# Output projection in three products of split operands, narrower heads of V, shared buffers and three moved steps in a transformer layer

## The reference

```python
q = x @ wq + x @ Aq @ Bq * 4; k = x @ wk; v = x @ wv + x @ Av @ Bv * 4   # 16 heads of 16
q, k = apply_rope(q), apply_rope(k)
attn = softmax(where(causal, -1e9, q @ k.T / 4))
x = layernorm(x + (attn @ v) @ wo)
h = gelu(butterfly(x @ W_exp + b_exp, up_weights) + up_bias)             # 1024 wide
x = layernorm(x + butterfly(h, down_weights) @ W_con + b_con + down_bias)
```

## Time and profile before

| what | value |
|---|---|
| median of 3 runs | 1165.44 us (1160.27 to 1165.82) |
| the profiled execution | 1159.63 us |
| its span | 1157.8 us |
| mean granted TensorE clock | 0.962 of full speed |
| PE, DVE, ACT, POOL busy | 1060.2, 875.7, 722.2, 570.2 us |
| 16 DMA engines | 147 GB/s on average |

### The profile page before, as it was taken

How to read it: one execution, slowest core, us unless ns; L and a number is a source line. 1 busy time by engine, 2 the same in 40 slices (tenths; PEclk the granted TensorE clock), 3 DMA queues, 4 the chain that set the end, 5 groups by cost and what they waited for, 6 DMA issues and landing times.

```text
span 1157.8 us, 28819 instructions
## 1 busy us (share of the span) xinstructions
PE 1060.2 (92%) x8974; PEld 787.9 (68%) x8974; DVE 875.7 (76%) x1950; ACT 722.2 (62%) x1113; POOL 570.2 (49%) x567
## 2 busy tenths in 40 slices
PE   5687879999999999999999999999999999999877
PEld 4464556767677776768677776768677776767566
DVE  6679977787777878787777778787777778776445
ACT  2186649475775758575775758575775758474613
POOL 2443526456382736456382836456382736443311
PEclk8788889999999999999999999999999999998989
DMA  7765553746465573646465573656465573651211
GB/s 275 158 207 117 163 131 93 197 122 193 98 211 129 160 185 117 192 118 201 91 210 129 154 192 113 194 117 193 99 212 129 155 190 111 195 124 52 67 37 37
DMA packets 95016, 169.91 MB, mean 147 GB/s; under 512 B 14904, under 2 KB 36152, under 8 KB 94976
## 3 DMA queue, kind: packets, MB, share of 16 engines
q1 hardware_dynamic: 93920, 166.53, 53.0%
q10 hardware_dynamic: 832, 1.83, 0.4%
q0 software_dynamic: 224, 1.04, 0.3%
HBM read 92.28 MB, written 77.07 MB: 146 GB/s over the span
## 4 chain that ended last, share of the span: by engine, by line
PE 63%; DVE 14%; ACT 8%; DMA 8%; issue 5%; SPq 1%; POOL 0%; ACTq 0%; DVEq 0%; POOLq 0%
PE ps_m L647 20%; PE ps_m L775 11%; PE ps_m L809 8%; PE ps_m L701 6%; PE ps_m L814 5%; PE ps_m L784 4%; PE ps_t L744 4%; DVE m_raw L1011 4%; DVE g_lo L484 4%; DMA m_scr<-small 2%; ACT pT L884 2%; PE ps_m L730 2%; DVE x1T L1056 2%; ACT gact L960 2%; DMA k_st<-qk_scr 1%
## 5 line engine op out<-in xcount | busy, mean ns | idle before, releaser
L884 ACT ACTIVATE pT<-ps_t 128x512 f32<-128x512 f32 x640 | 330.1, 604 | 250.8 <-PE ps_t L744 250.5
L1197 POOL TENSOR_SCALAR_AFFINE_SELECT pT<-pT 128x512 f32<-128x512 f32 (+1 forms) x320 | 193.4, 609 | 378.8 <-ACT pT L884 376.4
L1011 DVE TENSOR_REDUCE m_raw<-ps_m 128x1 f32<-128x512 f32 (+2 forms) x768 | 338.4, 503 | 22.4 <-PE ps_m L730 21.5
L701 PE MATMUL ps_m<-k_st,q_st 48*128 48x512 f32 (+3 forms) x1024 | 155.3, 359 | 37.7 <-DMA k_st<-qk_scr 7.8
L775 PE MATMUL ps_m<-pT,v_aug 128*32 128x512 f32 (+3 forms) x2048 | 154.9, 444 | 3.6 <-DVE m_raw L1011 3.2
L701 PEld LDWEIGHTS ps_m<-k_st,q_st 48*128 48x128 f32 x1024 | 88.7, 191 | 96.3 <-issue 47.6
L647 PE MATMUL ps_m<-x1T,w_hi 128*128 128x512 f32 x512 | 152.3, 404 | 1.6 <-ACT x1T L916 1.0
L744 PE MATMUL ps_t<-q_st,k_st 50*128 50x512 f32 (+3 forms) x1024 | 125.0, 351 | 5.7 <-DMA q_st<-m_scr 4.3
L775 PEld LDWEIGHTS ps_m<-pT,v_aug 128*32 128x32 f32 x2048 | 58.7, 111 | 82.0 <-issue 74.6
L647 PEld LDWEIGHTS ps_m<-x1T,w_hi 128*128 128x128 f32 x512 | 94.4, 189 | 25.8 <-issue 2.2
L814 PE MATMUL ps_m<-w_hi,g_lo 128*128 128x256 f32 x512 | 84.0, 287 | 6.6 <-DVE g_lo L484 6.5
(11 more groups left out here) (127 smaller groups left out, 2097.0 us busy)
## 6 DMA issues: line engine op xcount, KB each, us to landing
qk_scr<-rot_hi SPq DMA_DIRECT2D x62, 512.0 KB, 4.8
q_st<-qk_scr SPq DMA_DIRECT2D x128, 192.0 KB, 4.4
k_st<-qk_scr SPq DMA_DIRECT2D x128, 192.0 KB, 4.8
qk_scr<-rot SPq DMA_DIRECT2D x32, 512.0 KB, 5.4
o_scr<-o_raw SPq DMA_DIRECT2D x64, 256.0 KB, 3.8
r_b<-in_xT SPq DMA_DIRECT2D x17, 512.0 KB, 5.2
o_c<-o_scr SPq DMA_DIRECT2D x32, 256.0 KB
r_b<-r_scr SPq DMA_DIRECT2D x32, 256.0 KB
```

Source lines behind the costliest of these rows:

```text
L701: return pe.matmul(scores[r][:, off:off + (qt + 1) * P], q_st[rows, pr, qt * P:(qt + 1) * P], k_st[rows, pr, 0:(qt + 1) * P], start=start, ...
L884: act.activation(pT[:, slot, half * T:(half + 1) * T], ps_t[:, ST_BANK[2 * n + r], :], ACT.Exp, scale=SCALE).then_inc(exp_done, 1)
L1011: ins = dve.tensor_reduce(m_raw[:, g % 2, r, u // 2, qt:qt + 1], scores[:, off:off + (qt + 1) * P], AX.X, ALU.max, negate=True)
L1197: pool.affine_select(out=v, in_=v, compare_op=ALU.is_ge, fill=0.0, base=0, pattern=pattern, channel_multiplier=-1).then_inc(mask_done, 1)
```

## The change

- `v_aug` becomes a row of 17 columns per head (16 of V, one of ones). PV's weights are still 32 columns: those of the head and 15 of the next one, whose output rows nobody reads.
- WO runs with F32R operands in three products: o_hi by wo_hi, o_hi by wo_lo, o_lo by wo_hi. `wo` is split once at the start: ACT makes wo_hi, DVE wo_lo (in `WV`, step 3 of iteration -1).
- New steps of each batch: `HIO` 0 and 1 on ACT (o_hi from o_c), `LOO` 0 on POOL and `LOO` 1 on DVE (o_lo). HIO 0 and LOO 0 stand in step 3 after ON 1, HIO 1 and LOO 1 in step 4: HIO 1 ahead of PV 0, LOO 1 after MT 2 and ahead of the score units.
- `o_hi` lies in the memory of `rope_in`, `o_lo` in that of `o_c`; wo comes in through `pT`.
- V 0 moves from the front of step 2 to between its two score units, and DVE copies it to v_new instead of ACT.
- In step 3 the first halves of W2 0 and 1 come first, then their second halves, then the two additions.
- In `finish()` PV 3 of the last batch, with its copy and DMA, goes ahead of W1 5 and 6; HIO 0 and LOO 0 of the last batch come after LO 2 and 3, HIO 1 and LOO 1 after ON 1.

```diff
@@ finish
-        all_of("GE", y, 0) + all_of("W1", y, 5, 6) + all_of("PV", z, 3) + all_of("OE", z, 3) +
-        all_of("RAW", z, 3) + all_of("HI", y, 0) + all_of("W1", y, 7) + all_of("LO", y, 0, 1) +
+        all_of("GE", y, 0) + all_of("PV", z, 3) + all_of("OE", z, 3) + all_of("RAW", z, 3) +
+        all_of("W1", y, 5, 6) + all_of("HI", y, 0) + all_of("W1", y, 7) + all_of("LO", y, 0, 1) +
...
-        second(y, 0) + second(y, 1) + all_of("ON", z, 1) +
+        all_of("HIO", z, 0) + all_of("LOO", z, 0) +
+        second(y, 0) + second(y, 1) + all_of("ON", z, 1) + all_of("HIO", z, 1) + all_of("LOO", z, 1) +
@@ steps, early(p), p == 2
             put("REC", i - 1, 1)
-            if not static or i >= 0:
-                gemm("V", i + 1, 0)
             put("HI", i - 2, 1)
@@ p == 3
-            gemm("W2", i - 2, 0)
-            gemm("W2", i - 2, 1)
+            put("W2", i - 2, 0)
+            put("W2", i - 2, 1)
+            put("W2B", i - 2, 0)
+            put("W2B", i - 2, 1)
+            put("W2E", i - 2, 0)
+            put("W2E", i - 2, 1)
             put("BIAS", i - 2, 1)
             put("ON", i - 1, 1)
+            put("HIO", i - 1, 0)
+            put("LOO", i - 1, 0)
             put("XRES", i - 1, 1)
@@ p == 4
             put("QKL", i + 1, 1)
+            put("HIO", i - 1, 1)
             gemm("PV", i, 0)
             gemm("MT", i, 2)
+            put("LOO", i - 1, 1)
@@ between(p)
+        if p == 2 and (not static or i >= 0):
+            gemm("V", i + 1, 0)
@@ buffers
-        rope_in = sb("rope_in", [P, 2, T])
+        with ExitStack() as before_o_hi:
+            rope_in = before_o_hi.enter_context(nc.sbuf_tensor("rope_in", [P, 2, T], FP32))
+        o_hi = sb("o_hi", [P, 2, T], F32R)
-        v_aug = sb("v_aug", [P, NT, H, 2 * DH])
+        v_aug = sb("v_aug", [P, NT, VROW])
-        o_c = sb("o_c", [P, 2, T])
+        with ExitStack() as before_o_lo:
+            o_c = before_o_lo.enter_context(nc.sbuf_tensor("o_c", [P, 2, T], FP32))
+        o_lo = sb("o_lo", [P, 2, T], F32R)
@@ DVE and POOL, called for LOO 1 and LOO 0
+        def o_low(eng, b, n):
+            eng.wait_ge(oh_done, 2 * b + n + 1)
+            eng.tensor_tensor(o_lo[:, n, :], o_c[:, n, :], o_hi[:, n, :].bitcast(FP32), ALU.subtract)\
+               .then_inc(ol_done[n], 1)
@@ PE, WO
+                    pe.wait_ge(oh_done, 2 * b + 2)
...
+                    for o, w in ((o_hi, wo_hi), (o_hi, wo_lo), (o_lo, wo_hi)):
+                        if o is o_lo:
+                            for s in ol_done:
+                                pe.wait_ge(s, b + 1)
+                        for j in range(2):
+                            t = 2 * n + j
+                            for k in range(KD):
+                                mm = pe.matmul(pm[:, j * D:(j + 1) * D], o[:, k, t * P:(t + 1) * P], w[:, k, :],
...
@@ ACT
+                elif kind == "HIO":
+                    act.wait_ge(on_done, 2 * b + n + 1)
+                    wait(act, done["WO"], 2 * b)
+                    act.activation(o_hi[:, n, :], o_c[:, n, :], ACT.Copy).then_inc(oh_done, 1)
@@ DVE
+                elif kind == "V" and not n:
+                    dve.wait_ge(done["V"], 2 * b + 1)
+                    wait(dve, vcopy, b)
+                    dve.tensor_copy(v_new[:, 0:2, :].rearrange("p a c -> p (a c)"), pm).then_inc(evac_v[0], 1)
```

More of the change, by code:

```diff
@@ L28 @@
 NK = 3 * DH
+VH = DH + 1
+VROW = VH * H + DH - 1
 NM = 2
@@ L344, in layer @@
         w1_lo = sb("w1_lo", [P, KD, HID], F32R)
-        wo = sb("wo", [P, KD, D])
+        wo_hi = sb("wo_hi", [P, KD, D], F32R)
+        wo_lo = sb("wo_lo", [P, KD, D], F32R)
         bias_out = sb("bias_out", [P, D])
@@ L408, in layer @@
         oc_in = [sem(f"oc{n}_in") for n in range(2)]
+        oh_done, ol_done = sem("o_hi_done"), [sem(f"o_lo{n}_done") for n in range(2)]
         rb_in, on_done = [sem(f"rb{n}_in") for n in range(2)], sem("on_done")
@@ L655, in evacuated @@
                     wait(pe, max_done, 2 * (NU * b + n) + r + 1)
+                elif kind == "V":
+                    wait(pe, evac_v[n], b + 1)
                 elif kind == "W1":
@@ L779, in one @@
                 elif kind == "WO":
[L780 to L783, removed]
-                            mm = pe.matmul(pm[:, j * D:(j + 1) * D], o_c[:, k, t * P:(t + 1) * P],
-                                           wo[:, k, :], start=(k == 0), stop=(k == KD - 1))
+                    pe.wait_ge(oh_done, 2 * b + 2)
+                    if isinstance(b, int) and (b, n) == (0, 0):
+                        pe.wait_ge(w_lo, 3)
+                    for o, w in ((o_hi, wo_hi), (o_hi, wo_lo), (o_lo, wo_hi)):
[6 more added lines that the diff above has]
+                                mm = pe.matmul(pm[:, j * D:(j + 1) * D], o[:, k, t * P:(t + 1) * P], w[:, k, :],
+                                               start=(w is wo_hi and o is o_hi and j == 0 and k == 0),
+                                               stop=(o is o_lo and k == KD - 1), skip_group_check=True)
                     mm.then_inc(done["WO"], 1)
@@ L898, in one @@
                     act.activation(wv_hi[:, :, :], wv, ACT.Copy).then_inc(w_hi, 1)
+                    act.wait_ge(c_in, DMA * 4)
+                    act.activation(wo_hi[:, :, :], wo, ACT.Copy).then_inc(w_hi, 1)
                 elif kind == "VC":
                     wait(act, done["PV"], NG * b)
-                    act.wait_ge(evac["V"], 2 * b + 2)
+                    for s in evac_v:
+                        act.wait_ge(s, b + 1)
                     act.wait_ge(pool_c, 1)
-                    act.activation(v_aug[:, :, :, 0:DH],
+                    heads = v_aug[:, :, 0:VH * H].rearrange("p a (h d) -> p a h d", h=H)
+                    act.activation(heads[:, :, :, 0:DH],
                                    v_new[:, :, :].rearrange("p a (h d) -> p a h d", h=H), ACT.Copy)\
@@ L1133, in one @@
                                       ALU.subtract).then_inc(evac["DM"], 1)
+                elif kind == "LOO" and n:
+                    o_low(dve, b, n)
                 elif kind == "LO" and lows_on(b, n) == nc.vector:
@@ L1200, in one @@
                     rot_low(pool, b, n)
+                elif kind == "LOO" and not n:
+                    o_low(pool, b, n)
                 elif kind == "LO" and lows_on(b, n) == nc.gpsimd:
```

14 lines of the change are left out of this document (9 added, 5 removed).

## The result

The changed kernel takes 1169.28 us in the median of 19 runs (1164.78 to 1176.37); the kernel before, run beside it, takes 1161.18 (1152.88 to 1168.63, also 19 runs). The ratio is 1.0081 with an interval of 1.0059 to 1.0103: slower by some 0.8%, 7 to 12 us. So I read the mechanism from this trace, and sizes only where many iterations agree.

What follows compares the result with a forecast made beforehand. PE sets the 65 us period, with DVE equally a bound in steps 4 to 6. 14 batches of 0.85 (11.9), +0.3 for batch 14 and +1.8 for the end gave +14 on 1165.4, stated as 1178; range 1158 to 1187.

Steps and rivals of the forecast that it cites:

- B: Rival for LOO 1 in step 4: the lock doesn't bind or LOO 1 gets in first, +7, 1172 us; chance 0.17.
- C: Rival: PE's gain is used where r_b is early and the two cancel, within 5 us of before, 1165; chance 0.13.
- DVE and PE are bounds together in steps 4 to 6: From MT's copies to W2 of tile 2 DVE has no gap, so a 0.98 us delay there passes to W2.
- LOO 1 and its lock: Step 4: DVE's LOO 1 waits for POOL's whole subtraction, ends near 670.8, and the maxima begin 0.98 us late.
- so 0.85 a batch: Iteration growth from late maxima behind LOO 1: 0.98 us in the iteration read, 0.85 a batch on average.
- WO: Output projection in three products: 24 F32R matmuls take 2.85 us instead of 3.71, giving PE 0.86 a batch.
- V 0: Steps 2 and 3: v_new and g_lo waits go, a 0.9 us maximum wait comes; PE 0.3 to 0.5 earlier, worth nothing.
- The copy of PV 0: Step 4 on ACT: behind HIO 1 the copy ends near 670.2 instead of 669.7, without making PE later.
- 17 columns: PV's heads: weight loads and the copy to v_aug keep their sizes; nothing expected, at most a tenth on the copy.
- The end: Last batch: later reciprocal despite earlier PV 3, HIO 1 adding 0.7, WO about 5 us; together +1.8, bounds 0 and +3.
- rival D: PE's longer pauses, near 1.5 us in the iterations, bring its clock down: 25 us more, 1190; chance 0.05.
- A: Rival in steps 4 to 6: DVE has room, its statistics slip and the maxima keep their time; 18 less, 1147; chance 0.12.

Runs made afterwards that it cites:

- e1: The changed kernel with LOO 1 moved from DVE to POOL, right behind LOO 0: 1162.08 us, ratio 1.0017.
- e5: The kernel before with the two LN statistics ahead of WO 0's addition moved from step 4 to step 6: 1159.41 us, ratio 0.999.
- e3: The kernel before with only the moves of V 0 and W2 and DVE's copy of V 0: 1159.64 us, ratio 1.0025.
- e7: The changed kernel with LOO 1 on POOL, HIO 0 and LOO 0 ahead of ON 1, step 4's LN statistics in step 6, before's end: 1162.28 us.
- e8: The kernel of e7 with the changed end, PV 3 of the last batch ahead of W1 5 and 6: 1164.23 us, ratio 1.0039.
- e6: The changed kernel with the two LN statistics ahead of WO 0's addition moved from step 4 to step 6: 1164.24 us, ratio 1.005.
- e12: The kernel of e7 with HIO 1 behind PV 0, LNS 0 behind WO 1, and step 5's score tiles by query ahead of the transposed ones: 1160.2 us.
- e9: The kernel before with W2 2 moved from step 6 to right behind WO 1: 1203.64 us, ratio 1.0368.
- e4: The changed kernel with V 0 (still copied by DVE), W2's pieces and the end ordered as before: 1173.58 us, ratio 1.0112.

## Why the prediction was right, and where it was not

The forecast was 1178 us in a range of 1158 to 1187, slower with a chance of 0.69. It is slower, 1169.28, inside the range. The sign and its cause came as forecast, the size did not: the forecast stood on an old median of 1165.4; against the 1161.2 of the runs beside it, it said +12.6 and got +8.1. Its own bounds were +9 to +19 (1174 to 1184); that the time lies in the stated range is due to the room which that gave to rivals B and C, and B's +7 is nearer than the +14 of the sum. (The sum itself was off by one: 1165.4 + 14 is 1179.4, not 1178.) By its steps:

**DVE and PE are bounds together in steps 4 to 6: right**, and it is the point that decided. DVE has no gap from 677.71 on, the delay of the maxima goes through to W2 less 0.09 us, and e1 shows that without LOO 1 on DVE the iteration is 65.12.

**LOO 1 and its lock: right in mechanism, too large.** The term "so 0.85 a batch" measured 0.53; it is the mis-sized one. The chain that holds the changed kernel runs through ON 1. From the end of ON 1 to W2 2 the prediction had 7.90 us for the iteration that it read (668.90 to 676.8), where the kernel before has 6.90. Measured are 7.65 (677.48 to 685.13) and 7.66 in the mean. Two parts make the difference. LOO 1 ends 1.78 us after ON 1 and not 1.90, since it ends 0.54 after POOL's subtraction and not its own whole 0.66; and from the first maxima to W2 2 it is 5.94 us instead of 6.03, where I had counted on nothing. So in the mean this piece grew from 7.02 to 7.66, by 0.64 instead of 0.85. The remaining 0.10 lie between PV 3 and ON 1 (22.83 to 22.73), which the prediction left as it was; e5, which changes nothing there, has 22.69, so I don't put this part down to the change. In "SBUF — State Buffer", section "Who interferes with whom", the Trainium skill has the later of two such instructions blocked fully by the other; the trace agrees, with the restriction that a DVE instruction already started ends 0.54 us after POOL's, less than its whole 0.67.

**WO: 2.85 us predicted, 3.11 measured** from its first start to its last end, the measure in which it was 3.71; PE gets 0.6 and not 0.86. Hardly any of it reaches the period. From WO's start to W2 2's it is 5.07 us instead of 5.16: the 0.09 is all that is left. Predicted was a wait for a maximum's bank and one for the x1 addition, "together over 1.5 us a batch"; they are there, but 0.72 and 0.22 to 0.26. That is 0.5 less than forecast, and fits the two terms above: WO is 0.26 us longer than forecast, and W2 2 comes 0.25 earlier.

**V 0: half wrong.** The wait on v_new is gone and so is the one on g_lo, as predicted. The 0.9 us of wait on a maximum does not appear; in its place a transposed tile waits 0.48 for ACT's exponentials (663.59). PE reaches that tile over 1 us later than I counted (665.64, against the end of the reciprocal at 664.74; I had it 0.2 ahead of that end), 0.48 of it by this wait; the rest I have not taken apart. That the whole is worth nothing in the end was right for the changed kernel: PE is earlier at step 4 by 0.23 us (QK 3 to PV 0 is 14.42 instead of 14.65; forecast 0.3 to 0.5), and WO follows ON 1 and not MT 2. Alone, in e3, the moves give 0.11 an iteration.

**The copy of PV 0: right**, 0.53 us later; that no one behind it is late holds in eight of ten iterations, in the other two PE waits for it, 0.6 us together. **17 columns: right**; PV takes 2.36 us in both, the weight load 110 ns and the copy to v_aug 1.088 us against 1.080. This part was not run by itself.

**The end: +1.8 predicted, and not shown.** The reciprocal was forecast 1.3 us later by the queue; in e1, where PV 3 has its full clock, it is just that (39.8 after 38.5), in after 3.0 by the low clock of PV 3. PV 3 itself ends 1.5 us after the last mask in e1, forecast 1.4. HIO 1 adds 0.66 (forecast 0.7), WO takes 5.46 (forecast about 5). But from the reciprocal to ON 1 the traces differ by up to 2.8 us (8.4 in e1, 11.2 in before), and behind WO 15 by 5 us with the clock, more than the whole forecast. The medians of e7 and e8, which differ in the order of the end alone, give +2 with wide intervals. I had put a lower clock after a pause of 1.5 us at 0.05 (rival D) and only for the iterations; there it did not come (the granted clock from WO 3 to WO 14 is 1.00), but at the end of this trace it did, ahead of the last PV 3, and not at the same place in e1 and e8.

**The rivals.** A (DVE has room) is out: DVE's statistics are what doesn't slip, because they stand ahead of the addition, and e6 shows what it would take. B (the lock doesn't bind) is out by the durations of LOO 1, over 0.67 in nine of eleven iterations, though its price of 0.37 a batch is nearer to what came than mine. C would need PE to use its gain, and no run shows it doing so.

**What stays open.** Where a gain of WO would have to go is not settled in full. Between MT 2 and the first transposed tile of step 5 three things are level within about half a microsecond: DVE's row of work (5.9 us from MT 2 to that tile in before, 6.2 after), the round trip of m_scr through HBM, and r_b with HIO and LOO behind it. e1 relieved the first, e7 the first and parts of the third, e12 all three a little, and each time PE waited for another one. Which of them holds e12 was not tried.

## What to carry to other kernels

A shorter product is worth something only where PE and nothing else sets the stretch around it: look for the engine that is without a gap there before paying it with work for that engine. Here 0.6 us of PE were bought with 0.9 us of DVE in the one stretch of the iteration where DVE has none to give. And a step that looks idle may be somebody's cover: before W2 is moved, ask what PE would wait for at the place that it leaves.

## What the runs showed of the hardware

**Two subtractions on DVE and POOL, both operands in SBUF,** don't run side by side: POOL's takes its 1.28 us, and DVE's, begun meanwhile, ends 0.54 us after it. It goes both ways: ON 0 on POOL takes 2.24 us instead of 1.28 where DVE makes g_lo, and the last subtraction of o_lo on POOL, at 1117.7 beside g_lo, 1.99 (the maximum in the row of L514).

**The same pause doesn't always bring the same clock.** In the changed kernel PV 3 waits 1.78 us and then takes 4.05; in e1, at the same place after the same pause, it takes 2.36 (timeline of PE in e1):

```profile
1094.32 2.36 PE L801 MATMUL ps_m<-pT,v_aug 128*32 128x512 f32 x32 [1.78 <-POOL pT L1244]
```

In e8 it is 1.77 and 2.36. In e9, 1.77 us of waiting is followed by a clock of about 0.6 in nine of ten iterations and by 1.00 in one, at a difference of 1.5 us. At the end, the stretch behind the last WO takes 44.5 us at a clock of 0.96 and 49.6 at 0.81. That is more than half of what the change costs in all, and a reason not to read the end of a single trace.

**A small transfer took longer where a large one was issued closer ahead of it:** the write of m_scr 3.02 us in e7 (1.04 us behind the large one) from its issue to the issue that waits for it, 2.32 in before (2.54 behind it), 1.93 in e4 (2.92 behind it), in the mean of ten iterations. That the distance is the cause was not tested by itself.
